# Third layer's cross attention: query projection in three rounded passes, weights split by GpSimd in four pieces, and idle products in the two grouped attentions

## The reference

```python
def _L2_xattn_ref(hidden_q, kv_c, Wq, w_kc_q, w_kc_kv, W_qr, W_kr, Wo):
    DIM_Q, H, K, D_C, D_CQ, R = (256, 16, 128, 64, 192, 64)
    q_hk = (hidden_q @ Wq.T).reshape(Bv, Sv, H, K)
    q_big = jnp.einsum('bshk,hkq->bshq', q_hk, w_kc_q)      # 192 wide for each of 16 heads
    q_big = _apply_rope(q_big, sin_q, cos_q)
    kv_r = _apply_rope(kv_c, sin_k, cos_k)
    q_r = jnp.einsum('bshq,hqr->bhsr', q_big, W_qr)
    k_r = jnp.einsum('bld,hdr->bhlr', kv_r, W_kr)
    attn = jax.nn.softmax(jnp.einsum('bhsr,bhlr->bhsl', q_r, k_r), axis=-1)
    ctx_c = jnp.einsum('bhsl,bld->bhsd', attn, kv_r)
    ctx_lat = jnp.einsum('bhsd,hkd->bhsk', ctx_c, w_kc_kv)
    return ctx @ Wo.T
```

## Time and profile before

| what | value |
|---|---|
| median of 3 runs | 1545.8 us (1541.27, 1545.8, 1548.3) |
| the profiled execution | 1540.76 us, of which 1538.8 us are the span of the profile |
| mean granted TensorE clock of the profiled execution | 0.915 |
| grouped attentions, loop of the blocks | from about 257 and from about 1413 us |
| third layer's cross attention: `fold_cross` | about 875 to 908 us |
| its pipeline, first product of the projection to the last | 908.7 to 1068.5 us |
| its output product starts | 1099 us |

### The profile page before, as it was taken

The page is one execution under the profiler, slowest core; times in us unless marked ns, Lnnn a source line. Parts: engine busy times, 40 slices in busy tenths (PEclk is TensorE's granted clock), DMA queues, the critical chain, the costliest instruction groups (busy, mean ns, idle before and its releaser), DMA issues. The chain is left out here.

```text
span 1538.8 us, 28753 instructions
## 1 busy us (share of the span) xinstructions
PE 1343.5 (87%) x12013; PEld 1014.3 (66%) x12013; DVE 798.8 (52%) x1490; ACT 572.7 (37%) x1039; POOL 412.2 (27%) x335
## 2 busy tenths in 40 slices
PE   7769997989989978899979899999779579978988
PEld 3348995557967667688847667888665235656555
DVE  6734454555254652433428656877246448833442
ACT  3411323465544563433422421223324314541451
POOL 0153422005640000454410013333001219822000
PEclk9769998889999998999978899999889789989889
DMA  3000002108014000000081060000045200000000
GB/s 106 0 1 4 4 4 80 32 19 191 1 31 156 1 1 9 23 1 1 1 222 66 10 221 1 1 1 1 1 158 158 67 17 1 1 1 28 1 1 28
DMA packets 75041, 63.57 MB, mean 41 GB/s; under 512 B 21016, under 2 KB 72929, under 8 KB 74785
## 3 DMA queue, kind: packets, MB, share of 16 engines
q1 hardware_dynamic: 74144, 59.63, 13.6%
q0 software_dynamic: 768, 2.10, 0.4%
HBM read 53.33 MB, written 8.39 MB: 40 GB/s over the span
## 5 line engine op out<-in xcount | busy, mean ns | idle before, releaser
L1707 PE MATMUL ps<-rounded 128*128 128x512 f32 x384 | 92.7, 397 | 5.9 <-DVE work L1839 5.3
L1134 PE MATMUL ps<-fixed,work 128*128 128x256 f32 x384 | 91.0, 387 | 4.5 <-DVE weights L1160 2.4
L1183 POOL TENSOR_TENSOR fixed<-fixed,weights 128x768 f32<-128x768 f32 x32 | 57.9, 1810 | 129.2 <-DVE weights L1164 129.2
L1393 POOL TENSOR_TENSOR work<-weights,work 32x512 f32<-32x512 f32 x64 | 85.6, 1338 | 23.4 <-ACT work L1372 19.7
L1707 PEld LDWEIGHTS ps<-rounded 128*128 128x128 f32 x384 | 72.0, 191 | 24.5 <-issue 6.3
L1134 PEld LDWEIGHTS ps<-fixed,work 128*128 128x128 f32 x384 | 70.3, 190 | 18.0 <-DVE weights L1160 6.9
L1738 POOL TENSOR_TENSOR rounded<-weights,rounded 128x256 fp32r<-128x256 f32 x32 | 23.6, 760 | 204.4 <-ACT rounded L1756 204.4
L210 PE MATMUL ps<-fixed 128*128 128x128 f32 x160 | 36.1, 356 | 44.7 <-ACT fixed L198 38.7
L633 ACT COPY weights<-ps 64x512 f32<-64x512 f32 x96 | 55.6, 579 | 25.9 <-PE ps L592 24.1
L614 PE MATMUL ps<-work,weights 128*128 128x256 f32 x256 | 59.7, 395 | 5.0 <-ACT weights L633 5.0
L697 DVE TENSOR_TENSOR fixed<-fixed,ps 128x512 f32<-128x512 f32 x12 | 8.3, 688 | 99.8 <-PE ps L614 99.8
(11 more groups left out here) (447 smaller groups left out, 3278.4 us busy)
## 6 DMA issues: line engine op xcount, KB each, us to landing
weights<-in_L_ffn_masksT SPq DMA_DIRECT2D x32, 256.0 KB, 5.7
weights<-in_L_ffn_fc_w SPq DMA_DIRECT2D x16, 256.0 KB
weights<-in_L_xattn_Wq SPq DMA_DIRECT2D x2, 2048.0 KB, 10.1
weights<-in_L_xattn_WoT SPq DMA_DIRECT2D x2, 2048.0 KB, 10.4
sorted_in<-work SPq DMA_DIRECT2D x1, 3072.0 KB, 11.5
work<-sorted_in SPq DMA_DIRECT2D x12, 256.0 KB, 2.9
sorted_out<-work SPq DMA_DIRECT2D x12, 256.0 KB, 2.2
weights<-in_L_ffn_Wg SPq DMA_DIRECT2D x8, 256.0 KB, 5.9
```

The source lines that it names most:

```text
L1134: last = nc.tensor.matmul(seen[:, a, :], qf[:, c, u, a, :], k.hT[:, c, part * D:(part + 1) * D], start=c == 0, stop=c == KC - 1)
L1183: nc.gpsimd.tensor_tensor(ro[:, v % 2, :, :], ro[:, v % 2, :, :], sn, ALU.add).then_inc(s["roped"], 1)
L1393: last = nc.gpsimd.tensor_tensor(qb[64 + 32 * half:96 + 32 * half, 2 * (u % 2) + e, tok], cs[made, v % 2, :], sn[made, v % 2, :], ALU.add)
L1707: last = nc.tensor.matmul(ps[:, 2 * (n % 2) + i, :], a[:, q % 2, i, c, :], b[:, c, half * BANK:(half + 1) * BANK], start=c == 0 and part = ...
```

## The change

Three things change.

1. **The projection in three passes.** Weights and input are each split into a rounded part and a rest, both in the type float32r: `w_top`, `w_rest`, `h_top`, `h_rest`. `project(v)` makes 18 products (`w_top` with `h_top`, `w_top` with `h_rest`, `w_rest` with `h_top`, for three tiles and two chunks) in place of 6 in float32. ACT makes the rounded copies: the input in four quarters and the first pair's weights at the start of the stage, and the next pair's weights (768 columns) once for each pair. The rests of the input and of the first pair's weights are made by DVE at the start. The rests of each further pair's weights are made by POOL, in four pieces of 192 columns, one behind its sum of each quarter. All of `project` of a pair waits until all four pieces are there.
2. **Room.** Rows of `qf` that have been split hold the context later (`Pieces`), the probabilities lie where `k.hT` was, the loaded weights of the stage are given up after `fold_cross`, and the table of the rotation moves to the fixed region. The tiles' names change with it (`cross`, `rounded` in place of `weights`).
3. **Idle products.** In both grouped attentions `hold` gives six bf16 products after scores(0, 0) and three after ask(1), into a bank that is not in use then.

```diff
@@ stage_gqa, PE @@
                 if t < NT:
                     scores(t, 0)
+                if t == 0:
+                    hold(k, 4, 6)
...
                 if t + 1 < NT:
                     ask(t + 1)
+                if t == 0:
+                    hold(k, 4, 3)
@@ the cross attention's second part @@
         def project(pe, v):
             u, part = divmod(v, 4)
+            pe.wait_ge(s["w_rest"], 4 * u + 4)
+            if u == 0:
+                pe.wait_ge(s["h_rest"], part + 1)
             for a in range(3):
                 if v and a != 1:
                     pe.wait_ge(s["sined"], 3 * v - 2 if a == 0 else 3 * v)
                 for c in range(KC):
-                    last = nc.tensor.matmul(seen[:, a, :], qf[:, c, u, a, :], k.hT[:, c, part * D:(part + 1) * D],
-                                            start=c == 0, stop=c == KC - 1)
+                    for n, (m, of) in enumerate(((w_top, h_top), (w_top, h_rest), (w_rest, h_top))):
+                        last = nc.tensor.matmul(seen[:, a, :], m[:, u % 2, c, a, :], of[:, c, part * D:(part + 1) * D],
+                                                start=c == 0 and n == 0, stop=c == KC - 1 and n == 2)
...
         def dve_q(dve, v):
+            if v == 0:
+                rest_of_rows(dve, 0)
+                dve.wait_ge(s["w_top"], 1)
+                for part in range(4):
+                    rest_of_weights(nc.vector, 0, part)
+                for part in range(1, 4):
+                    rest_of_rows(dve, part)
             dve.wait_ge(s["q_proj"], v + 1)
...
+        def round_weights(act, u):
+            if u >= 2:
+                act.wait_ge(s["q_proj"], 4 * u - 4)
+            nc.scalar.copy(whole(w_top[:, u % 2]), whole(qf[:, u])).then_inc(s["w_top"], 1)
+
+        def round_rows(act, part):
+            nc.scalar.copy(quarter(h_top, part), quarter(k.hT, part)).then_inc(s["h_top"], 1)
+
+        def rest_of_rows(dve, part):
+            dve.wait_ge(s["h_top"], part + 1)
+            nc.vector.tensor_tensor(quarter(h_rest, part), quarter(k.hT, part), quarter(h_top, part), ALU.subtract).then_inc(s["h_rest"], 1)
+
+        def rest_of_weights(ops, u, part):
+            cols = slice(192 * part, 192 * part + 192)
+            ops.tensor_tensor(whole(w_rest[:, u % 2])[:, cols], whole(qf[:, u])[:, cols], whole(w_top[:, u % 2])[:, cols],
+                              ALU.subtract).then_inc(s["w_rest"], 1)
...
         def act_q(act, h):
-            if h:
+            if h == 0:
+                round_rows(act, 0)
+                round_weights(act, 0)
+                for part in range(1, 4):
+                    round_rows(act, part)
+            else:
                 copy_q(act, 2 * h - 1)
+
+        def act_b(act, h):
+            if h % 2 == 0 and h // 2 + 1 < NH // 2:
+                round_weights(act, h // 2 + 1)
+            copy_q(act, 2 * h)
@@ POOL @@
                 nc.gpsimd.tensor_tensor(ro[:, v % 2, :, :], ro[:, v % 2, :, :], sn, ALU.add).then_inc(s["roped"], 1)
+                u, part = divmod(v, 4)
+                if u + 1 < NH // 2:
+                    if part == 0:
+                        pool.wait_ge(s["w_top"], u + 2)
+                        if u:
+                            pool.wait_ge(s["q_proj"], 4 * u)
+                    rest_of_weights(nc.gpsimd, u + 1, part)
```

More of the change, by code:

```diff
@@ L29 @@
 I32 = mybir.dt.int32
-W_COLS = (16256, 2056, 8488, 16776, 15384, 2312, 16256, 16384, 16128, 2056, 2064)
+W_COLS = (16256, 2056, 8488, 16776, 15384, 2312, 14976, 16384, 16128, 2056, 2064)
 STAGES = list(range(11))
@@ L525, with __init__, __getitem__ @@
 NH, DH = 16, 64
+class Pieces:
+    def __init__(self, *pieces):
+        self.pieces = pieces
+    def __getitem__(self, key):
+        rows, u, cols = key
+        for piece in self.pieces:
+            if u < piece.shape[1]:
+                return piece[rows, u, cols]
+            u -= piece.shape[1]
 class Latent:
@@ L629, in copy_context @@
             act.wait_ge(s["pv"], u + 1)
+            q_hooks.get("ctx", none)(act, u)
             for jj in range(2):
@@ L707, in load_latent_cross @@
     if L == "L2_xattn_":
-        w.table = r.take(2, 3, SEQ)
+        w.table = k.fixed.take(2, 3, SEQ)
     w.wq = r.take(NH, D)
@@ L841, in _ @@
                 made = ps[:, 3 + e, 0:384].rearrange("p (c q) -> p c q", c=2)
-                nc.vector.tensor_copy(qf[:, :, h // 2, 0:2, 64 * e:64 * e + 64], made.rearrange("p c (a q) -> p c a q", a=2)[:, :, :, 0:64])
-                nc.vector.tensor_copy(qf[:, :, h // 2, 2, :].rearrange("p c (a e q) -> p c a e q", a=2, e=2)[:, :, :, e],
+                nc.vector.tensor_copy(qf[:, h // 2, :, 0:2, 64 * e:64 * e + 64], made.rearrange("p c (a q) -> p c a q", a=2)[:, :, :, 0:64])
+                nc.vector.tensor_copy(qf[:, h // 2, :, 2, :].rearrange("p c (a e q) -> p c a e q", a=2, e=2)[:, :, :, e],
                                       made.rearrange("p c (a q) -> p c a q", a=2)[:, :, :, 64:96]).then_inc(s["qfs"], 1)
@@ L1108, in stage_L2_xattn @@
     k.work.clear()
-    qf = k.work.take(KC, NH // 2, 3, P)
+    qf = k.work.take(NH // 2, KC, 3, P)
     pm = k.work.take(NH // 2, D)
@@ L1112, in stage_L2_xattn @@
     c1 = k.work.take(NH // 2, 3, P)
-    w.region.at = 2 * 3 * SEQ
-    kk = w.region.take(TOK)
+    kk = k.work.take(TOK)
     f = Named()
@@ L1117, in stage_L2_xattn, with attend_L2 @@
     fold_cross(k, w, f, c1, qf)
-    t = Latent(w.region, w.region, kk, kvt, pm, w.region)
-    qb = w.region.take(2, TOK)
-    sn = w.region.take(3, D)
+    k.release()
+    with ExitStack() as room:
+        cols, rounded_cols = 7424, 7168
+        more = Region(room.enter_context(nc.sbuf_tensor("cross_2", [P, cols], F32, side="left")), cols)
+        rounded = Region(room.enter_context(nc.sbuf_tensor("rounded_6", [P, rounded_cols], F32R, side="left")), rounded_cols)
+        attend_L2(k, w, qf, pm, kvt, c1, kk, more, rounded)
+def attend_L2(k, w, qf, pm, kvt, c1, kk, more, rounded):
+    nc, ps = k.nc, k.ps
+    t = Named()
+    t.kk, t.kvt, t.pm = kk, kvt, pm
+    own = qf.rearrange("p u c a q -> p (u c a q)").rearrange("p (u n) -> p u n", n=TOK)
+    t.ctxT = Pieces(own, more.take(2, TOK))
+    t.pT = more.take(2, 2, 4, P)
+    t.pr = Region(k.hT.rearrange("p c t -> p (c t)"), KC * TOK).take(3, NT, SEQ)
+    t.mx, t.sm, t.rs = more.take(2, NT), more.take(2, NT), more.take(2, NT)
+    qb = more.take(2, TOK)
+    sn = more.take(3, D)
+    h_top, h_rest = rounded.take(KC, TOK, dt=F32R), rounded.take(KC, TOK, dt=F32R)
+    w_top, w_rest = rounded.take(2, KC, 3, P, dt=F32R), rounded.take(2, KC, 3, P, dt=F32R)
+    whole = lambda t: t.rearrange("p c a q -> p (c a q)")
+    quarter = lambda t, part: t[:, :, part * D:(part + 1) * D]
     ro = k.h.rearrange("p j d -> p (j d)")[:, 0:6 * D].rearrange("p (n a t) -> p n a t", n=2, a=3)
@@ L1126, in stage_L2_xattn @@
                       ap=[list(swapped.ap[0]), [-D, 2]] + [list(e) for e in swapped.ap[2:]])
-    with k.stage("cosed", "sined", "roped", *CORE_SEMS) as (block, s):
+    with k.stage("h_top", "h_rest", "w_top", "w_rest", "cosed", "sined", "roped", *CORE_SEMS) as (block, s):
         def project(pe, v):
             u, part = divmod(v, 4)
+            pe.wait_ge(s["w_rest"], 4 * u + 4)
+            if u == 0:
+                pe.wait_ge(s["h_rest"], part + 1)
             for a in range(3):
@@ L1165, in dve_q, with own_rows_read @@
                                         bc(w.table[here, 1, 2, :], 1, 4), ALU.mult).then_inc(s["sined"], 1)
+        def round_weights(act, u):
[11 more added lines that the diff above has]
+                              ALU.subtract).then_inc(s["w_rest"], 1)
+        def own_rows_read(act, u):
+            if u < 6:
+                act.wait_ge(s["w_rest"], 4 * ((TOK * u + TOK - 1) // (KC * 3 * P)) + 4)
         def copy_q(act, v):
@@ L1187, in stage_L2_xattn @@
                {"pe": lambda pe, h: pe_q(pe, 2 * h), "pe_b": lambda pe, h: pe_q(pe, 2 * h + 1),
-                "act": act_q, "act_b": lambda act, h: copy_q(act, 2 * h),
+                "act": act_q, "act_b": act_b, "ctx": own_rows_read,
                 "dve": lambda dve, h: dve_q(dve, 2 * h), "dve_b": lambda dve, h: dve_q(dve, 2 * h + 1), "ready": lambda h: 4 * (h // 2) + 4,
@@ L3060, in decoder @@
         k.nc, k.dram, k.serial, k.former = nc, dram, 0, []
-        total, fixed_cols = 53200, 7872
+        total, fixed_cols = 53200, 8256
         arena = ctx.enter_context(nc.sbuf_tensor("fixed", [P, fixed_cols], F32))
@@ L3098, in decoder @@
             with ExitStack() as room:
-                k.work = Region(room.enter_context(nc.sbuf_tensor(f"work_{n}", [P, work_cols - rounded], F32)), work_cols - rounded)
+                k.work = Region(room.enter_context(nc.sbuf_tensor(f"work_{n}", [P, work_cols - rounded], F32, side=("right", "left")[n % 2])), work_cols - rounded)
                 k.spare = k.work
@@ L3102, in decoder @@
```

(1 more changed line is left out.)

## The result

| | changed kernel | kernel before |
|---|---|---|
| median, 13 runs each | 1552.7 us (from 1549.1 us) | 1544.4 us (1538.5 to 1554.5) |
| ratio of the two | 1.0054, 95% interval 1.0036 to 1.0072 | |
| profiled execution: own time, span | 1550.5, 1548.8 us | as ahead of the prediction |

One run of the changed kernel took 1914.7 us with a granted clock of 0.65, and is left out of the ratio. The change costs 0.54%: 8.4 us, between 5.6 and 11.1. The forecast was 1549.0 in a range of 1537 to 1560, +2.9 us. The sign is as forecast, and so are the parts but for the clock's in the pipeline; the sum is some 5 us too low.

The account below looks back on a forecast made before the run. PE, with DVE near, was taken to bound the cross attention's full phase, and half clock to slow the grouped attentions. Pipeline +7.1 and start +2.3 give +9.4; +4.3 clock, -10.8 idle products: +2.9, so 1549 us, range 1537 to 1560.

Parts of the forecast that it names:

- the clock's in the pipeline: Cross attention: half clock after four idle stretches of PE adds 1.1 us each, +4.3 us, bounds 0 to 9.
- the projection: Cross attention's `project`: 18 records take 2.32 us, 0.52 less than before.
- Rival D: Cross attention's projection takes 1.97 us, 0.20 less on some twenty PE-bound steps: -4, so 1545 us; chance 0.05.
- the new wait: Step to the next pair: PE's projection waits for POOL's fourth piece; 7.9 us in place of 6.11 in full phase.
- steps in the full phase: Cross attention: a pair's steps take 4.70, 4.96, 4.4 and 7.9 us, the pair 21.95 in place of 21.21.
- the pipeline without clock: Cross attention: 31 steps take 164.1 us in place of 157.05, +7.1 us.
- The start: Start of the cross attention: ACT's roundings and DVE's pieces make the first cosines 2.3 us later.
- the idle products: Both grouped attentions: the clock stays full, -5.7 and -5.1, together -10.8 us, bounds 0 and -12.
- B: Slower: idle products don't hold the clock in one or both grouped attentions; 1554.5 to 1559.5 us; chance 0.23.
- E: Idle products have no effect, nor has idle time on the cross attention's clock; 1555 us; chance 0.05.
- Rival A: The forecast itself: the projection's waits and the kept clock cancel; 1543 to 1555 us; chance 0.52.

Follow-up runs that it names:

- the three others: Changed kernel without any idle products (1562.2 us), with the six idle products alone (1550.1 us), and with the three alone (1557.3 us).
- the warm waits: Changed kernel plus idle bf16 products at the end of weight folding and ahead of the first projections of pairs 0 to 3: 1542.8 us, ratio 1.0018.

## Why the prediction came out as it did

**Right: the projection.** Forecast 2.32 us for 18 records, measured 2.38 to 2.42; with a record of 0.283 that is (2.38 - 0.283)/17 = 0.123 from one to the next. Rival D falls. The rule behind it (the Trainium skill, TensorE: Matmul & The Clock Gate, "Back-to-back issue gap") would give an estimate of 17 x 0.109 + 0.283 = 2.14 us; the measurement decides. That section itself says that its formula is for a product alone, and that in a stream with a weight load for each product both set the spacing, which is the case here.

**Right: the place and size of the new wait.** Forecast steps in the full phase were 4.70, 4.96, 4.4 and 7.9, measured 4.71, 5.02, 4.50 and 7.92. DVE goes ahead of the piece, and the second step is bound by DVE. The idle time of PE at these places was priced somewhat high: 4.0 us ahead of pairs 1 to 3 and 2.1 ahead of the others, measured 3.07 to 3.75 and 1.67.

**Slightly low: the pipeline without clock.** Forecast 164.1 us for 31 steps, measured 165.87 at full clock. Of the 1.8 missing, 5 x 0.18 come from full pairs (22.13 in place of 21.95), 0.2 from the last pair, and the rest from the steps of pairs 0 and 1, with 4.12 us in place of 3.98 and 4.1. The walk took the gap from sines to `project` from the kernel before, and it is 0.1 longer. The pipeline term is +8.8, forecast +7.1. The start is +2.2, forecast +2.3: PE idles 4.35 us in place of 1.77, and its projection is 0.4 shorter.

**The step that was mis-sized: "one projection at half clock costs 2.17 more ... I take 1.1 for each of the four".** The half clock cost 3.2 us in the pipeline in the profiled execution of the changed kernel, and 5.1, 6.1 and 6.2 in the three others; the first projection adds 1.2 in the one and 1.8 in the others (from its start to the first cosines 3.64 us, and 4.2 in the three, where it is 2.45 at full clock). Together 4.4 to 8.0 where 4.3 was forecast, inside its bounds of 0 to 9. The changed kernel's profile agrees with 4.3, but it is the cheapest of the four; their mean is 6.8, and by medians the warm waits are worth 5.6. The middle should have stood at 6 or 7, which is 2 of the 5 us that the sum lacks; another 1.7 are the steps.

**Right: the idle products.** Forecast -10.8, measured -5.4 - 4.7 = -10.1 in the profile and -9.4 by medians. Rivals B and E fall.

**The sum again.** +8.8 + 2.2 + (4.4 to 8.0) - 10.1 = +5.3 to +8.9, measured +8.4 (5.6 to 11.1). Rival A holds in its mechanism: waits and kept clock nearly cancel, and more is left than forecast. The time itself, 1549.0 forecast and 1552.7 measured, comes out 1.8 us nearer than the change does (2.9 and 8.4, 5.5 apart); most of that is luck, since the prediction started from a median of three runs, 1545.8, and thirteen give 1544.4.

**What stays open.** The two profiles differ by 10.0 us of span, of which 4.7 lie in code that the change leaves alone. The profile of before had 632.5 us from `scores(2, 0)` of the first attention to the first cosines; with the idle products alone it was 634.5, though nothing in between is changed there. No experiment settles whether that is scatter; the medians don't need it.

## What to carry to other kernels

Work that is moved to an idle engine should be issued so that its last piece is not behind the last thing that engine does for the same deadline: GpSimd was busy 28% of the time, and yet it makes 22 us where four pieces of 0.6 us stand in its queue. The whole change is 8 us slower than before or, with the pieces early, 14 us faster. A new wait of TensorE is to be priced twice, once as the wait and once as half clock in what follows, with a range for the second, since waits of the same length were followed by either clock. A pause ahead of narrow products is worth filling with idle ones if it stands where the clock falls; fill the first such pause, and look whether later ones still matter.

## What the runs showed of the hardware that was not expected

- Waits of the same length were followed by either clock: at the same place in two kernels, 3.45 us and a projection of 2.40, 3.44 us and one of 3.10; and inside one execution 3.29 us and 2.42, 3.31 us and 4.21.
- Six idle products in a pause of 1.41 us (1.47 us of PE) saved 5.4 us behind it.
- Between two queued GpSimd instructions a DVE instruction came in that was issued during the first, and the second took 1.04 us in place of 0.596.
- Products in float32r on 256 columns, each with its own weight load, follow each other at 0.123 us at full clock.
